# Attention of a gated cross-attention and mixture-of-experts layer: six units a round in place of eight, on one core

## The reference, cut to what matters

```
scores = jnp.einsum('bnghd,bmgd->bnghm', q, k) / scale
scores = jnp.where(causal, scores, NEG_INF)
attn = jax.nn.softmax(scores, axis=-1)
out = jnp.einsum('bnghm,bmgd->bnghd', attn, v).reshape(B, S, D)
```

## Time and profile before

| | us |
|---|---|
| median of 3 runs | 1301.37 (1299.77 to 1302.19) |
| profiled execution | 1302.34 |
| its span | 1300.5 |
| attention stage within the span | about 117 to 396 |
| PE, DVE, ACT, POOL busy over the span | 1246.3, 648.9, 592.8, 632.4 |
| granted TensorE clock, mean over the span | 0.987 |

### The profile page before, as it was taken

How to read it: one execution, slowest core, us unless ns; L and a number is a source line. 1 busy time by engine, 2 the same in 40 slices (tenths; PEclk the granted TensorE clock), 3 DMA queues, 4 the chain that set the end, 5 groups by cost and what they waited for, 6 DMA issues and landing times. The chain is left out here.

```text
span 1300.5 us, 24058 instructions
## 1 busy us (share of the span) xinstructions
PE 1246.3 (96%) x7963; PEld 907.7 (70%) x7964; DVE 648.9 (50%) x1831; ACT 592.8 (46%) x1050; POOL 632.4 (49%) x726
## 2 busy tenths in 40 slices
PE   8999999999998999999999899999999999999995
PEld 5554444444444347686867699999999999999994
DVE  5346999999894665753704213333333333342200
ACT  2222777777772134222222255555555555555552
POOL 6010333333343242444345266766666766766663
PEclk8999999999999998999999999999999999999998
DMA  9453433333335313101022355555655666665343
GB/s 348 153 163 104 140 107 111 104 114 108 111 99 165 117 46 149 41 25 57 9 68 96 111 132 117 122 127 139 159 127 137 162 169 142 159 147 138 74 73 41
DMA packets 73889, 153.19 MB, mean 118 GB/s; under 512 B 10724, under 2 KB 16356, under 8 KB 73048
## 3 DMA queue, kind: packets, MB, share of 16 engines
q1 hardware_dynamic: 52776, 102.37, 24.3%
q0 software_dynamic: 21040, 49.88, 18.6%
HBM read 97.56 MB, written 52.23 MB: 115 GB/s over the span
## 5 line engine op out<-in xcount | busy, mean ns | idle before, releaser
L641 DVE CUSTOM_DVE_ANT_0 a_mb<-a_mb,late 128x128 f32<-128x128 f32 x480 | 226.2, 515 | 29.7 <-PE a_mb L682 22.8
L1520 DVE CAST e_w<-e_w 128x480 fp32r<-128x480 f32 x135 | 76.1, 564 | 300.1 <-DMA e_w<-in_w2T 295.9
L627 ACT ACTIVATE a_at<-a_eb 128x1024 f32<-128x1024 f32 (+3 forms) x256 | 179.7, 705 | 61.6 <-PE a_eb L695 54.7
L558 POOL TENSOR_SCALAR_AFFINE_SELECT a_at<-a_at 128x256 f32<-128x256 f32 x256 | 104.6, 409 | 201.1 <-ACT a_at L627 198.8
L1673 PE MATMUL e_yps<-e_w,e_hT 128*128 x711 | 197.2, 404 | 0.9 <-ACT e_hT L1583 0.9
L1652 PE MATMUL e_up<-e_w,e_xT 128*128 x948 | 170.1, 328 | 0.0
L1652 PE MATMUL e_gate<-e_w,e_xT 128*128 x948 | 167.7, 325 | 1.0 <-issue 1.0
L1652 PEld LDWEIGHTS e_gate<-e_w,e_xT 128*128 128x128 f32 x948 | 155.7, 189 | 11.3 <-issue 6.5
L1652 PEld LDWEIGHTS e_up<-e_w,e_xT 128*128 128x128 f32 x948 | 149.2, 188 | 0.0
L1673 PEld LDWEIGHTS e_yps<-e_w,e_hT 128*128 128x128 f32 x711 | 128.1, 189 | 25.5 <-issue 1.2
L1549 POOL TENSOR_TENSOR e_hT<-e_hc,e_hT 128x384 fp32r<-128x384 f32 x79 | 83.7, 1060 | 112.0 <-ACT e_hc L1584 111.8
(11 more groups left out here) (261 smaller groups left out, 1787.4 us busy)
## 6 DMA issues: line engine op xcount, KB each, us to landing
e_w<-in_w13T SPq DMA_DIRECT2D x16, 1408.0 KB
dq<-p_parts SPq DMA_DIRECT2D x32, 256.0 KB, 2.4
a_q<-dq SPq DMA_DIRECT2D x64, 128.0 KB
do<-a_o SPq DMA_DIRECT2D x32, 256.0 KB, 2.0
e_w<-in_w2T SPq DMA_DIRECT2D x16, 512.0 KB
a_k<-dk SPq DMA_DIRECT2D x64, 98.0 KB
e_w<-in_ctxT SPq DMA_DIRECT2D x4, 1024.0 KB, 14.1
e_w<-in_x SPq DMA_DIRECT2D x4, 1024.0 KB, 13.2
```

The source lines that it names most:

```text
L558: eng.affine_select(out=square, in_=square, compare_op=ALU.is_ge, fill=0.0, base=0, pattern=[[0, 2], [1, P]], channel_multiplier=-1).then_ ...
L627: eng.activation(at[i % 2][:, ch, 2 * hp:2 * hp + 2, ch * P:SEQ], eb[u % 2][:, :, ch * P:SEQ], ACT.Exp, scale=0.25).then_inc(s_exp, 1)
L641: eng.tensor_tensor_reduce(out=b[:, 0:w], in0=b[:, 0:w], in1=io["late"][:, SEQ - w:SEQ], scale=1.0, scalar=3 * NEG, op0=ALU.add, op1=ALU.m ...
```

## The change

Units and fills are cut anew.

- UNITS has six entries (ch, js). Chunks 0 and 1 keep one unit for each j; chunks 2 and 3 have one unit each for both j (BOTH). In these, one product for each t streams two blocks of 256 queries into one bank, and one exponential takes all four heads (1024 elements per partition for chunk 2, 512 for chunk 3). POOL clears four squares in one instruction there.
- FILLS replaces PAIRS and ORDER in this stage: a bank is filled with chunk 3, or chunk 2, or with chunks 1 and 0 side by side (256 columns each). Six entries, each for t=0 and t=1, are twelve fills a round for the same sixteen products and sixteen reductions. One increment of s_smax is made for a fill, and DVE waits once for it. Each of the two fills of an entry waits for its own bank: fill f waits for all reductions of the fills up to f-3. TAKEN counts reductions.
- VALUES, READY and FILL are fitted to six units. Two units have two pieces; the last piece of a result is still in the third unit.
- turn_row stands in the third unit between the score products and the value pieces, where it stood behind the second unit's value pieces. The wait for the row of maxima (s_row) has moved into open_unit.

```diff
--- before.py
+++ after.py
@@ -40,10 +40,12 @@
 AHEAD, RING = 2, 3
 SKIPPED, TURNED = HG, HG + 1
 PAIRS = (((0, 0), (1, 3)), ((0, 1), (1, 2)), ((1, 0), (0, 3)), ((1, 1), (0, 2)))
-ORDER = tuple((j, turn) for turn in range(4) for j in range(2))
-UNITS = ((0, 0), (3, 0), (0, 1), (3, 1), (1, 0), (2, 0), (1, 1), (2, 1))
-READY = {0: 2, 3: 3, 1: 6, 2: 7}
-VALUES = (((1, 1, 1, 3),), ((1, 2, 2, 4),), ((1, 1, 3, 4),), (), ((0, 0, 0, 2),), ((0, 0, 2, 3),), ((0, 0, 3, 4),), ((0, 3, 3, 4),))
+BOTH = (0, 1)
+UNITS = ((0, (0,)), (0, (1,)), (1, (0,)), (1, (1,)), (2, BOTH), (3, BOTH))
+READY = {0: 1, 1: 3, 2: 4, 3: 5}
+VALUES = (((1, 1, 1, 3),), ((1, 1, 3, 4), (1, 2, 2, 3)), ((1, 2, 3, 4), (1, 3, 3, 4)), (), ((0, 0, 0, 2),), ((0, 0, 2, 4),))
+FILLS = ((0, (3,)), (0, (1, 0)), (0, (2,)), (1, (2,)), (1, (3,)), (1, (1, 0)))
+TAKEN = tuple(itertools.accumulate((len(FILLS[n // 2][1]) for n in range(2 * len(FILLS))), initial=0))
 LD, ROWS = 6 * 16, 16
 CUTS = 8
 NI, NS = len(ICH), len(SCH)
@@ -517,7 +519,7 @@
 
 def stage_attend(nc, io, dram):
 
-    FILL, SEAM = (12, 12, 12, 12, 4, 4, 4, 4), 50
+    FILL, SEAM = (12, 12, 12, 12, 4, 4), 50
 
     with ExitStack() as c:
         sb = lambda n, s, d=F32: c.enter_context(nc.sbuf_tensor(n, s, d))
@@ -540,11 +542,17 @@
         block = c.enter_context(nc.Block())
         made = AHEAD * CH * HG + 1
 
-        def pair(i, p):
-
-            g = (i - AHEAD) * len(ORDER) + p
-            j, turn = ORDER[p]
-            return g, j, [(t, ch, mb[(2 * g + n) % RING]) for n, (t, ch) in enumerate(PAIRS[turn])]
+        def fill(i, u, t):
+
+            j, chunks = FILLS[u]
+            f = 2 * ((i - AHEAD) * len(FILLS) + u) + t
+            widths = [max(256, (ch + 1) * P) for ch in chunks]
+            return f, j, [(ch, mb[f % RING][:, sum(widths[:n]):sum(widths[:n + 1])]) for n, ch in enumerate(chunks)]
+
+        def taken(f):
+
+            rounds, n = divmod(f, 2 * len(FILLS))
+            return made + rounds * CH * HG + TAKEN[n]
 
         row = eb[1][0:HG * CH, 0, 0:P]
 
@@ -552,11 +560,11 @@
         def _(eng):
             begin(eng, s_causal)
             for i in range(NIT):
-                for u, (ch, hp) in enumerate(UNITS):
+                for u, (ch, js) in enumerate(UNITS):
                     eng.wait_ge(s_exp, i * len(UNITS) + u + 2)
-                    square = at[i % 2][:, ch, 2 * hp:2 * hp + 2, ch * P:(ch + 1) * P]
+                    square = at[i % 2][:, ch, 2 * js[0]:2 * js[-1] + 2, ch * P:(ch + 1) * P]
                     eng.affine_select(out=square, in_=square, compare_op=ALU.is_ge, fill=0.0, base=0,
-                                      pattern=[[0, 2], [1, P]], channel_multiplier=-1).then_inc(s_causal, 1)
+                                      pattern=[[0, 2 * len(js)], [1, P]], channel_multiplier=-1).then_inc(s_causal, 1)
 
         @block.sync
         def _(eng):
@@ -618,14 +626,17 @@
                 eng.activation(mrow[i % 2], row, ACT.Copy).then_inc(s_mr, 1)
 
             for i in range(NIT):
-                for u, (ch, hp) in enumerate(UNITS):
+                for u, (ch, js) in enumerate(UNITS):
                     if u == 2 and i + 1 < NIT:
                         copy_row(i + 1)
                     if u == 3 and i:
                         result(i - 1)
                     eng.wait_ge(s_sexp, i * len(UNITS) + u + 2)
-                    eng.activation(at[i % 2][:, ch, 2 * hp:2 * hp + 2, ch * P:SEQ], eb[u % 2][:, :, ch * P:SEQ],
-                                   ACT.Exp, scale=0.25).then_inc(s_exp, 1)
+                    to, scores = at[i % 2][:, ch, 2 * js[0]:2 * js[-1] + 2, ch * P:SEQ], eb[u % 2][:, :, ch * P:SEQ]
+                    if js == BOTH:
+                        to = to.rearrange("p (j t) n -> p t j n", j=2)
+                        scores = eb[u % 2][:].rearrange("p t (j n) -> p t j n", j=2)[:, :, :, ch * P - SEQ // 2:SEQ // 2]
+                    eng.activation(to, scores, ACT.Exp, scale=0.25).then_inc(s_exp, 1)
             result(NIT - 1)
 
         @block.vector
@@ -633,13 +644,14 @@
             begin(eng, s_split, io["s_triple"], io["s_inv"])
             for i in range(AHEAD, NIT):
                 eng.wait_ge(s_mt, i)
-                for p in range(len(ORDER)):
-                    g, j, products = pair(i, p)
-                    for n, (t, ch, b) in enumerate(products):
-                        w = (ch + 1) * P
-                        eng.wait_ge(s_smax, made + 2 * g + n + 1)
-                        eng.tensor_tensor_reduce(out=b[:, 0:w], in0=b[:, 0:w], in1=io["late"][:, SEQ - w:SEQ], scale=1.0, scalar=3 * NEG,
-                                                 op0=ALU.add, op1=ALU.max, accum_out=mx[i % 2][:, 2 * t + j, ch:ch + 1]).then_inc(s_rmax, 1)
+                for u in range(len(FILLS)):
+                    for t in range(2):
+                        f, j, products = fill(i, u, t)
+                        eng.wait_ge(s_smax, made + f + 1)
+                        for ch, b in products:
+                            w = (ch + 1) * P
+                            eng.tensor_tensor_reduce(out=b[:, 0:w], in0=b[:, 0:w], in1=io["late"][:, SEQ - w:SEQ], scale=1.0, scalar=3 * NEG,
+                                                     op0=ALU.add, op1=ALU.max, accum_out=mx[i % 2][:, 2 * t + j, ch:ch + 1]).then_inc(s_rmax, 1)
 
             eng.memset(three, 0.0).then_inc(s_split, 1)
             eng.wait_ge(s_split, 2)
@@ -673,27 +685,36 @@
                 for _ in range(n):
                     eng.matmul(at_bank[:, 0:P], io["onesb"], io["before"], start=True, stop=True)
 
-            def max_products(i, p):
-                g, j, products = pair(i, p)
-                r = i % NB
-                eng.wait_ge(s_rmax, made + 2 * g - 1)
-                for t, ch, b in products:
-                    rows, w = slice(HALF * t, HALF * t + ROW_MAX), max(256, (ch + 1) * P)
-                    eng.matmul(b[:, 0:w], q[r][rows, j, ch * P:(ch + 1) * P], k[r][rows, 0:w], start=True, stop=True).then_inc(s_smax, 1)
-
-            def exp_unit(i, u):
-                ch, j = UNITS[u]
-                r, n0, e = i % NB, min(ch * P, 256), i * len(UNITS) + u
+            def max_products(i, u, t):
+                f, j, products = fill(i, u, t)
+                r, rows = i % NB, slice(HALF * t, HALF * t + ROW_MAX)
+                if f >= RING:
+                    eng.wait_ge(s_rmax, taken(f - RING + 1))
+                else:
+                    eng.wait_ge(s_rmax, made)
+                for ch, b in products:
+                    mm = eng.matmul(b, q[r][rows, j, ch * P:(ch + 1) * P], k[r][rows, 0:b.shape[-1]], start=True, stop=True)
+                mm.then_inc(s_smax, 1)
+
+            def open_unit(i, u):
+
+                e = i * len(UNITS) + u
+                if u == 0:
+                    eng.wait_ge(s_row[i % NB], ROWS * (i // NB + 1))
                 if e >= 2:
                     eng.wait_ge(s_exp, e)
                 if u == 3 and i + 1 < NIT:
                     eng.wait_ge(s_mr, i + 3)
                 if i == 0 and u >= 4:
                     spin(eb[u % 2][:, 1], FILL[u])
-                for t in range(2):
-                    rows = slice(HALF * t, HALF * t + ROW_MAX + 1)
-                    mm = eng.matmul(eb[u % 2][:, t, n0:SEQ], k[r][rows, ch * P:(ch + 1) * P], q[r][rows, j, n0:SEQ], start=True, stop=True)
-                mm.then_inc(s_sexp, 1)
+
+            def exp_products(i, u, t):
+                ch, js = UNITS[u]
+                r, n0, rows = i % NB, min(ch * P, 256), slice(HALF * t, HALF * t + ROW_MAX + 1)
+                keys = k[r][rows, ch * P:(ch + 1) * P]
+                if js == BOTH:
+                    return eng.matmul(eb[u % 2][:, t, :].rearrange("p (j n) -> p j n", j=2), keys, q[r][rows, :, n0:SEQ], start=True, stop=True)
+                return eng.matmul(eb[u % 2][:, t, n0:SEQ], keys, q[r][rows, js[0], n0:SEQ], start=True, stop=True)
 
             def turn_row(i):
 
@@ -707,6 +728,7 @@
                     of, cols = i - late, slice(n0 * P, n1 * P)
                     if not 0 <= of < NIT:
                         continue
+                    last = (late, ch, n0, n1) == VALUES[2][-1]
                     if n0 == ch:
                         eng.wait_ge(s_causal, of * len(UNITS) + READY[ch] + 2)
                         if ch == 0:
@@ -716,8 +738,8 @@
                         for t in range(2):
                             h = 2 * t + j
                             mm = eng.matmul(pv[32 * h:32 * h + 32, cols], v[of % NB][:, ch, :], at[of % 2][:, ch, 2 * j + t, cols],
-                                            start=ch == 0 and n0 == 0, stop=(late, ch, n0, n1) == VALUES[2][0], skip_group_check=True, tile_position=(0, 32 * h))
-                    if (late, ch, n0, n1) == VALUES[2][0]:
+                                            start=ch == 0 and n0 == 0, stop=last, skip_group_check=True, tile_position=(0, 32 * h))
+                    if last:
```

(13 more changed lines are left out.)

## The result

The changed kernel took 1277.68 us (median of 4, 1277.22 to 1280.7), the kernel before 1301.26; the ratio is 0.9825 with a 95% interval of 0.9807 to 0.9843. The forecast was 1277. The profiled execution took 1277.22, its span is 1275.5. The same kernel in a later job took 1280.89 (4 runs, 1277.22 to 1281.14), ratio 0.9845 (0.9821 to 0.9868).

A forecast was written before the change was run, and what follows sets the result against it. PE and DVE, neither full, coupled through three banks, were taken as the bound. Rounds of 7.9 instead of 8.65 save 22.5 us over 30 rounds, 24.1 with the last two: 1277 us, 8-in-10 range 1267 to 1295.

The forecast's parts named there:

- the walk: One attention round followed through starts and releases of PE, DVE and ACT: the next round begins at 7.81 us.
- the seam: Where one round meets the next: between 0 and 0.20 us of wait stays, taken as 0.1.
- Round 0 and the tail: Round 0 saves 0.75 us like other rounds, its eight dropped fill matmuls left to the range; last two rounds save 1.6.
- The gain is in switches and stretches of PE, not in its waits.: Per attention round, PE's own work falls 0.76 us to 7.02, while stalls stay about as now at 0.84.
- the shorter chain itself is costed at nothing; it is covered by PE: ACT's four exponentials become two, at 1.02 and 0.60 us; counted as no gain, since ACT's chain never ends last.
- The wait of F9: F9, a fill of unit 4, stands at PE's head until its bank is free: 0.65 us stall a round.
- DVE's own work: Four reductions each of 128, 256, 384 and 512 columns, at 0.22, 0.35, 0.51 and 0.65: 6.92 us a round.
- the stall goes too: Rival: DVE keeps up, F9 never waits and PE alone sets the round at 7.1 us: 1253, chance 0.08.
- The transpose: Behind unit 2's scores, it needs unit 1's exponential: 0.04 us stall.
- Three products in a row in one row half: Two units with chunks 1 and 0: weight loads taken as hidden; rival in line, 0.29 more each, 1294.5, chance 0.15.
- Two-block products: Scores of units 4 and 5: taken as no extra; rival 0.64 us more each, 1316, chance 0.12 including similar costs.
- it does not do what it says: Rival: the loop stays paced by the exchange over three banks, at 8.6 us a round: 1300, chance 0.07.

The follow-up runs named there:

- eight_units: The changed kernel with the scores of chunks 2 and 3 split by j again, eight units, six pairs of fills kept: 8.33 a round, 1292.13 us.
- early_fill: The changed kernel with the t=0 fill of unit 3 issued in unit 2, behind its scores and ahead of the transpose: 1267.45 us.
- level_pairs: The kernel before with only its pairs cut anew, so both row halves get equal chunks: 9.07 a round, 1319.48 us.
- six_alone: The changed kernel's six units, value pieces and transpose with the eight pairs of the kernel before: 8.98 a round at full clock, 1442.84 us.
- row_back: The changed kernel with the transpose put back behind the second unit's value pieces: 8.33 to 8.38 a round at full clock, 1312.14 us.
- late_fill: The changed kernel with the second fill of unit 4 issued behind that unit's scores instead of ahead: 7.72 a round, 1270.8 us.
- early_behind: The changed kernel with the t=0 fill of unit 3 issued in unit 2, behind the transpose and ahead of the value pieces: 1270.91 us.

## Why the prediction was right, point by point

- *Attention, by the walk.* Forecast 7.81 plus 0.1 for the seam, measured 7.80. Unit 0 was 1.33 instead of 1.22 (its second fill waits for a bank: that is the seam's wait), unit 1 1.36 instead of 1.44, unit 2 1.47 instead of 1.39, units 3 and 4 together 2.40 instead of 2.41, unit 5 1.24 instead of 1.35; the stall between the fills of unit 4 was 0.70. So the seam's 0.1 exists, but units 1 and 5 are shorter by 0.19 and unit 2 longer by 0.08, and the agreement of the walk with 7.80 comes in part from terms that cancel. On top of the walk the 0.1 made the forecast of the round too long; it cost 3 us of the sum.
- *Round 0 and the tail.* 2.0 and 2.2 gained, where I had 0.75 and 1.6.
- *So attention gave 28.7, not 24.1.* The total came out at the forecast since 2.5 less ahead of the stage and 6.2 more behind it left 25.0. Both go with the clock: 1.00 instead of 0.97 in the first 100 us, 0.89 instead of 0.96 in the closing stage. The agreement of the totals to 1 us is therefore partly luck; the step that failed is the silent one, that nothing outside the stage would move.
- *"The gain is in switches and stretches of PE, not in its waits."* As an account of after against before it holds: the stalls stayed near 0.8. As a cause it was incomplete. In eight_units PE has the shorter work too (the same fills and value pieces), and the round is only 0.32 shorter, because new waits take its place. The step that failed is "the shorter chain itself is costed at nothing; it is covered by PE": against eight units the merged ones are worth 0.5 to 0.6 of a round, in eight_units through the double buffer. This does not come on top of the forecast. The sum credits PE with 2 x 0.22 for two units fewer, and that amount stands for the same merging. Eight_units, where PE's own work is that of after, loses 0.53 all the same, so the term had about the right size and only in part the right cause.
- *The wait of F9* was where the walk put it, and its cause was in the main DVE's late start on the fill ahead (0.44 gap). That was the best lead of the walk: early_fill takes the wait away and 0.25 of the round with it.
- *DVE's own work* was mis-sized. The 0.22 and 0.35 for reductions of 128 and 256 columns are of reductions ahead of which DVE had stood idle, the 0.51 and 0.65 are not. In after, a reduction directly behind another holds up the next by 0.25, 0.38, 0.52 and 0.65, one behind a pause by 0.35, 0.48 and 0.62 (256, 384, 512), so four of each are up to 7.20 and not 6.92. The rival "the stall goes too", with DVE at 6.93 and a round of 7.1, could not have come true. Early_fill's 7.55 leaves DVE some 0.4 a round.
- *The transpose.* I had a stall of 0.04 at its new place; it is 0.16, since an exponential's end reached PE 0.14 later and not 0.06. At its old place it would have cost 0.71.
- *Three products in a row in one row half.* Unit 5 takes 225.93 - 225.25 = 0.68, where 0.78 was forecast with hidden weights and 1.07 with weights in line; 0.22 + 1024/2400 is 0.65. The rule of the Trainium skill (TensorE: Matmul & The Clock Gate, Part 3, "The mechanism"), that weights load under a running matmul only for other rows, taken alone would give the longer one; the measurement decides against it for these products.
- *Two-block products* cost nothing here: unit 4, 224.01 to 224.68, takes 0.67, as the 512+512 unit of before did (224.73 to 225.40).
- *The rival "it does not do what it says"* took the exchange over three banks for the bound. It is wrong for after, and right for level_pairs, where a pair waits for a wide reduction, and for six_alone, where two pairs a round follow another with too little for PE to do between.
- *The slower side* that I named (two blocks) was harmless. The one that exists is the clock: row_back lost some 14 us to it in attention (279.6 against 265) and six_alone some 130 (413.4 against 283 at 8.98 a round), and nothing in the trace of before, at 1.00 throughout the stage, pointed to it.

## What to carry to other kernels

Where two engines exchange buffers and neither is full, walk one round by starts and releases, not by busy shares: the walk found both the length of the round and the one fill whose earlier issue took another 6.6 us out of the stage. Keep the pieces handed over few: in eight_units two light units paid a trip of 1.17 through the double buffer with 0.7 of work to cover it. Look at which buffer each wait names, too: in level_pairs a wide reduction in first place cost more than equal halves gave. And test a part on its own before crediting it, since here two parts of -0.32 and +0.33 made -0.85 together, and compare stages before totals: late_fill (246.9 in attention, 1270.8) and early_behind (242.4, 1270.91) have the same total.

## What I had not expected of the hardware

- The granted clock of TensorE fell to half in the middle of the stage, behind stretches in which PE was busy 43.49 of 50 us (six_alone) and 47.52 of 52 (row_back). In six_alone it did not come back for the remaining stage, though PE was then busy 318.06 of 340 us at the lower level. In level_pairs, with PE busy 247.09 of 280 us at a round of 9.07, it did not fall. What decides stays open.
- The same closing stage, without a changed instruction, takes 100 to 107 us at mean clocks of 0.96 to 0.89, and after's two traces both show the longer one. That is 0.5% of the kernel, more than the runs of one job of after scatter (1277.22 to 1280.7).
- A reduction directly behind another takes 0.03 longer than one behind a pause, at every width seen both ways in after (0.38 against 0.35 at 256 columns, 0.52 against 0.48 at 384, 0.65 against 0.62 at 512). In level_pairs and before, a 128-wide one behind a pause took 0.22, in after one directly behind another 0.25. A sum of DVE's work has to take each from a row of its own kind.
